# Graph attention on one core: a table fetch by product for every third step's eighth tile, and 64-row edge products

## What is computed

```python
q, k, v = x @ Wq + bq, x @ Wk + bk, x @ Wv + bv
e = eattr @ We
kj = k[src] + e
alpha = sum(q[dst] * kj, axis=-1) / sqrt(C)
a = exp(alpha - segment_max(alpha, dst)[dst])
a = a / (segment_sum(a, dst)[dst] + 1e-16)
out = segment_sum(a[..., None] * (v[src] + e), dst) + x @ Ws + bs
```

## Time and profile before

| | |
|---|---|
| median of 3 runs | 6819.26 us (6818.12 to 6822.41) |
| profiled execution | 6818.34 us, its span 6816.5 us |
| mean granted clock of TensorE | 0.538 of full speed |
| busy: PE, PEld | 4422.8 us (65%), 3475.0 us (51%) |
| busy: DVE, ACT, POOL | 4366.3 us (64%), 1118.9 us (16%), 4726.5 us (69%) |
| DMA | 675.79 MB, mean 99 GB/s |

### The profile page before, as it was taken

The page is one execution under the profiler, slowest core; times in us unless marked ns, Lnnn a source line. Parts: engine busy times, 40 slices in busy tenths (PEclk is TensorE's granted clock), DMA queues, the critical chain, the costliest instruction groups (busy, mean ns, idle before and its releaser), DMA issues. The chain is left out here.

```text
span 6816.5 us, 149747 instructions
## 1 busy us (share of the span) xinstructions
PE 4422.8 (65%) x36620; PEld 3475.0 (51%) x36620; DVE 4366.3 (64%) x15732; ACT 1118.9 (16%) x4722; POOL 4726.5 (69%) x5116
## 2 busy tenths in 40 slices
PE   7996666666666667666666666667666666666665
PEld 5775444444444446444444444446444444444444
DVE  5556666666666666666666666666666666666666
ACT  3222111111111112111111111112111111111111
POOL 1224777777777775777777777775777777777776
PEclk9995555555555555555555555555555555555555
DMA  4553333333333333333333333333333333333333
GB/s 128 159 159 96 95 95 95 96 95 95 95 96 95 96 95 98 95 95 95 95 95 95 95 95 95 95 96 97 95 95 95 95 95 96 95 95 95 96 96 80
DMA packets 687682, 675.79 MB, mean 99 GB/s; under 512 B 369234, under 2 KB 506388, under 8 KB 687636
## 3 DMA queue, kind: packets, MB, share of 16 engines
q0 software_dynamic: 161600, 320.52, 18.3%
q1 hardware_dynamic: 496944, 301.76, 16.3%
q10 hardware_dynamic: 29092, 52.97, 2.6%
HBM read 652.96 MB, written 21.67 MB: 99 GB/s over the span
## 5 line engine op out<-in xcount | busy, mean ns | idle before, releaser
L1621 POOL DMA_INDIRECT Gall<-KV,sdn x4848 | 4590.0, 947 | 1517.0 <-issue 1380.9
L754 DVE TENSOR_TENSOR kj<-Gall,pE 128x512 f32<-128x512 f32 x603 | 414.4, 687 | 1973.4 <-DMA Gall<-KV,sdn 1971.3
L963 PE MATMUL pG<-O,vals 128*66 128x42 f32 (+1 forms) x10736 | 1291.9, 308 | 0.7 <-ACTq L1242 0.7
L963 PEld LDWEIGHTS pG<-O,vals 128*66 128x66 f32 (+1 forms) x10736 | 1200.8, 223 | 47.4 <-ACT vals L1002 28.4
L948 PE MATMUL pY<-fw,Ob 128*42 128x6 bf16 (+1 forms) x4800 | 255.1, 176 | 1139.9 <-DVE cr L807 1139.9
L994 ACT ACTIVATE vals<-dd 128x16 f32<-128x16 f32 (+1 forms) x606 | 131.6, 217 | 4679.5 <-DVE dd L834 4671.0
L948 PEld LDWEIGHTS pY<-fw,Ob 128*42 128x42 bf16 x4800 | 220.4, 121 | 1192.9 <-issue 1192.9
L896 PE MATMUL pE<-bd,ea 128*128 128x256 f32 x1212 | 739.9, 714 | 13.6 <-PEq L1242 13.6
L955 PEld LDWEIGHTS pM<-Mb,OTs 42*128 42x128 bf16 x4800 | 176.3, 101 | 921.1 <-issue 921.1
L901 PE MATMUL pE<-bd,ea 128*128 128x256 f32 x1212 | 642.8, 634 | 0.0
L955 PE MATMUL pM<-Mb,OTs 42*128 42x6 bf16 (+1 forms) x4800 | 209.9, 163 | 514.2 <-DVE df L825 511.8
(11 more groups left out here) (223 smaller groups left out, 6539.9 us busy)
## 6 DMA issues: line engine op xcount, KB each, us to landing
db<-D SPq DMA_DIRECT2D x606, 256.0 KB
ea<-in_ea SPq DMA_DIRECT2D x606, 128.0 KB
Gall<-KV,sdn POOLq DMA_INDIRECT x4848
db<-D ACTq DMA_DIRECT2D x202, 256.0 KB, 3.5
qw<-QT SPq DMA_DIRECT2D x1818, 5.2 KB
dr<-in_dr SPq DMA_DIRECT2D x1212, 4.0 KB
ea<-in_ea SPq DMA_DIRECT2D x202, 64.0 KB, 3.3
sdn<-in_sdn SPq DMA_DIRECT2D x606, 12.0 KB
```

Source lines behind the costliest of these rows:

```text
L754: return e.tensor_tensor(kj[:, :, :], G[u][:, :, 0:64], pE[u][:, :].rearrange("p (j c) -> p j c", c=64), ALU.add)
L963: return e.matmul(out[0:AR, 0:W], vals[u][:, j, 0:AR], O[u][:, j, :], start=j == 0, stop=j == T - 1)
L1621: e.indirect_dma_start(G[u][:, j, :], None, kvtab, bass.IndirectOffsetOnAxis(ap=sdn[u][:, j:j + 1], axis=0)).then_inc(s_g[u], 16)
```

## The change

- The table rows of k and v stay in SBUF too: `rows_A` writes into `KVS` [128, 50, 128] f32 instead of `stg`, and the stores to DRAM read from there. Scratch of the setup lies in `KVS` to make room.
- For steps of slot 0 from step 3 on (`picks`), POOL leaves out the gather of tile 7. PE makes these rows: `oh` is, for each group ("quad") of four table tiles, a one-hot matrix of the 128 keys against the row number; its product with 512 columns of `KVS` is accumulated in `pG` over all 13 quads. The 13 are spread as 4, 4 and 5 over three steps (`p_gp`, between `aT` and `Me`; the quad of the last two tiles has 256 columns). `v_oh` makes the one-hot matrices a step ahead, and `v_sel` takes, at the start of the picked step, of the four tiles in `pG` the right one into `G`.
- The keys: the mean pass collects the eighth source column of each step in `srcT`; before the first attention pass it is transposed, made into 16-bit keys and stored in `K16`, and SP loads the key row of a pick into `kb`.
- `agg` sums into `pY` instead of `pG`, and `facc` waits for `aT`.
- Edge products in attention passes: four of 128 columns, each over 64 rows, the two row halves into different banks of PSUM, so that `kj` and `vj` read `pE` through another pattern.

```diff
+        self.quads = -(-self.tiles // 4)
...
+    order_q = list(range(QUADS - 2)) + [QUADS - 1, QUADS - 2]
+    PIECE = [QUADS // 3, QUADS // 3, QUADS - 2 * (QUADS // 3)]
+    FROM = [0, PIECE[0], PIECE[0] + PIECE[1]]
...
+    KVS = sb("KVS", [128, NT, 128])
...
-            if before_kv[c]:
-                e.wait_ge(s_kv[g], before_kv[c])
             e.wait_ge(own["P"], pP["mm", c])
-            e.activation(stg[:, g, 0:m, 0:128], kv_bank[c % 2][:, 0:128 * m].rearrange("p (t c) -> p t c", t=m),
+            e.activation(KVS[:, cells(c), :], kv_bank[c % 2][:, 0:128 * m].rearrange("p (t c) -> p t c", t=m),
                          ACT.Copy).then_inc(own["A"], 1)
...
-                "V": ["A kj", "A vj", "B fhi", "B fm", "B flo", "B cr", "Z OT", "A prod", "A alpha", "C d1", "C d",
-                      "Z cont", "Z last", "A flag", "A O", "B X", "B Mhi", "B Mm", "B Mlo", "B df", "C vals",
+                "V": ["A sel", "A kj", "A vj", "B fhi", "B fm", "B flo", "B cr", "Z OT", "A prod", "A alpha", "C d1", "C d",
+                      "Z cont", "Z last", "A flag", "A O", "Z oh", "B X", "B Mhi", "B Mm", "B Mlo", "B df", "C vals",
                       "D facc", "D acc", "A scan"],
-                "P": ["B Fb", "A q", "D agg7", "B Mn", "Z e", "A aT", "B Me"],
+                "P": ["B Fb", "A q", "D agg7", "B Mn", "Z e", "A aT", "A gp", "B Me"],
...
-                "V": ["C acc", "Z O", "Z OT"],
+                "V": ["C acc", "Z src", "Z O", "Z OT"],
...
+        first_pick = 2 + z.peel
+        pick_slot = first_pick % 3
...
+        sums = [pSumY, pSumY, pSumY] if att else [pG, pQ, pY]
...
+        def picks(s):
+            return s.slot == pick_slot and not (isinstance(s.i, int) and s.c < first_pick)
...
+        def v_src(e, s):
+            ge16(e, s_i, 1, s)
+            return e.tensor_copy(srcT[:, bass.ds(s.value(), 1)], sdn[s.slot][:, LAST:T])
...
+        def v_sel(e, s, inc, n):
+            u = s.slot
+            to = G[u][:, LAST, :]
+            e.tensor_scalar(quarter[:, :], sdn[u][:, LAST:T], 7, 3, ALU.logical_shift_right,
+                            ALU.bitwise_and).then_inc(sel_V, 1)
+            e.wait_ge(sel_V, sel_at(s, 0))
+            e.tensor_tensor(msk[:, :], ioq[:, :], quarter[:, :].to_broadcast([128, 4]),
+                            ALU.is_equal).then_inc(sel_V, 1)
+            e.wait_ge(sel_V, sel_at(s, 1))
+            after(e, "P", "gp", s - 1)
+            e.tensor_scalar(to, pPick[:, 0, :], msk[:, 0:1], None, ALU.mult).then_inc(sel_V, 1)
+            for k in range(1, 4):
+                e.wait_ge(sel_V, sel_at(s, k + 1))
+                i = e.scalar_tensor_tensor(to, pPick[:, k, :], msk[:, k:k + 1], to, ALU.mult, ALU.add)
...
+        def v_oh(e, s):
+            k = (s.slot - pick_slot) % 3
+            m, f = PIECE[k], FROM[k]
+            if k == 0:
+                e.wait_ge(s_k, s.times(16, 16 * (2 - first_pick // 3)))
+            return e.scalar_tensor_tensor(
+                oh[s.slot][:, 0:m, :], kb[:, :].unsqueeze(1).to_broadcast([128, m, 128]), prow[:, 0:1],
+                pQd[:, f:f + m].unsqueeze(2).to_broadcast([128, m, 128]), ALU.subtract, ALU.is_equal)
...
+                after(e, "P", "aT", s + 3)
...
-                return e.matmul(pE[u][:, 0:256], ea[u][:, 0:128], bd32[:, l, :], start=True, stop=True)
...
+                return edges(e, u, 0)
...
+        def edges(e, u, half):
+            for x in range(2):
+                c = pEhalf[u][x] + 128 * half
+                p = e.matmul(pEall[:, c:c + 128], ea[u][64 * x:64 * x + 64, 128 * half:128 * half + 128],
+                             bd32[64 * x:64 * x + 64, l, 128 * x:128 * x + 128], start=True, stop=True)
+            return p
...
+        def p_gp(e, s):
+            k = (s.slot - pick_slot) % 3
+            after(e, "V", "oh", s)
+            hold(e)
+            if k == 0 and picks(s):
+                after(e, "V", "sel", s)
+                hold(e)
+            for n in range(PIECE[k]):
+                q = order_q[FROM[k] + n]
+                m = min(4, NT - 4 * q)
+                p = e.matmul(pG[:, 0:128 * m], oh[s.slot][:, n, :],
+                             KVS[:, 4 * q:4 * q + m, :].rearrange("p t c -> p (t c)"),
+                             start=k == 0 and n == 0, stop=k == 2 and n == PIECE[k] - 1)
+            return p
...
+            e.dma_start(kb[:, :], K16[bass.ds(s.value(), 1), :].to_broadcast([128, 128])).then_inc(s_k, 16)
...
-            for j in range(T):
+            for j in range(T - 1 if picks(s) else T):
```

More of the change, by code:

```diff
@@ L21 @@
 SL = 4
+LAST = T - 1
 class Sizes:
@@ L123, in build @@
     dnarrow = Gall[:, B * T:B * T + B * T // 2].bitcast(I16)
+    srcT = sb("srcT", [128, 4 * KG])
+    kb = sb("kb", [128, 128], I16)
+    oh = [sb(f"oh{u}", [128, PIECE[2], 128]) for u in range(3)]
+    quarter = sb("quarter", [128, 1], I32)
+    msk = sb("msk", [128, 4])
+    prow = sb("prow", [128, 1])
+    ioW = sb("ioW", [128, W])
+    ioq = sb("ioq", [128, 4], I32)
     sdn = [sb(f"sdn{u}", [128, 3 * T], I32) for u in range(3)]
@@ L551, in query_A @@
             e.wait_ge(own["P"], pP["qs", c])
-            e.activation(stg[:, g, 0:m, 128:192], both[:, :, 0:64], ACT.Copy).then_inc(own["A"], 1)
+            e.activation(stg[:, g, 0:m, :], both[:, :, 0:64], ACT.Copy).then_inc(own["A"], 1)
             e.activation(SQ[:, cells(c), :], both[:, :, 64:128], ACT.Copy).then_inc(own["A"], 1)
@@ L1242, in missing, with made @@
             e.sem_inc(prog[k], m - n)
+        def made(s):
+            return not isinstance(s.i, int) or s.c >= first_pick - 3
         def vector_step(e, t, on):
@@ L1379, in tensor_step @@
                 missing(e, "P", t, "aT", "aT")
+            if made(at):
+                p_gp(e, at).then_inc(pP, 1)
+            else:
+                missing(e, "P", t, "gp", "gp")
             if "B" in on:
@@ L1532, in load_db, with load_keys @@
             e.dma_start(db[u][:, :], D16[bass.ds(b, 1), :].to_broadcast([128, T * 128])).then_inc((s_l if att else s_d)[u], 16)
+        def load_keys(e, s):
+            if not (isinstance(s.i, int) and s.c == first_pick):
+                after(e, "V", "oh", s - 4)
+                hold(e)
+            e.dma_start(kb[:, :], K16[bass.ds(s.value(), 1), :].to_broadcast([128, 128])).then_inc(s_k, 16)
         def load_rows(e, s, b, base):
@@ L1576, in sync_step @@
             load_rows(e, s, b, base)
+            if att and picks(s + 2):
+                load_keys(e, s + 2)
         def sync(e, ready):
@@ L1588, in sync @@
                     sync_step(e, At(i, c))
+            if att:
+                after(e, "V", "oh", At(n, 1 + z.peel))
+                hold(e)
+                e.dma_start(kb[:, :], K16[0:1, :].to_broadcast([128, 128])).then_inc(s_k, 16)
         def pool_step(e, s):
```

179 lines of the change are left out of this document (129 added, 50 removed).

## The result

On the chip on which the kernel before takes 6818.86 us (median of 4 runs, 6818.12 to 6822.41), the changed kernel takes **6609.18 us** (4 runs, 6607.14 to 6612.21). The ratio is 0.9692, 95% interval 0.968 to 0.9704: 209.7 us less. The forecast was 6578.4, range 6560 to 6640. The profiled execution took 6607.14 us, 211.2 less than the one of before.

A forecast was written before the change was run, and what follows sets the result against it. The prediction took POOL's issue of gathers to bound the attention passes. From 6819.3 us it took 251.9 for the removed gathers and added 11 for setup and the ends of passes: 6578.4 us, range 6560 to 6640.

The forecast's parts named there:

- What bounds, and what a gather is worth: Attention passes: POOL's gather issue sets the pace; 201 gathers fewer at 1.253 us each save 251.9 us.
- The ends: Setup and the start and finish of passes: additions of +11 us together, bounds 0 to +25.
- The openings of the second and third pass: Start of these passes: one or two `oh` on the way to the first `kj`, +1 us each.
- The drains: End of each pass: the last `gp` and `sel` stand in the open, +1 us for each of three passes.
- TensorE: Attention steps: PE work of 9.15 us, or 8.7 with faster edges, under the 9.60 us step, hidden behind POOL.
- The block: Fetch products in each step: 7.1 us at the lower clock, which was to rise within each block; taken at 4.15.
- the second rival: Attention steps: the clock alternates and PE sets the pace at 10.3 us a step, 7002 us in all; chance 0.08.
- Edge products: Attention steps on PE: 2.0 us as now if pairs follow one another, 1.0 less if they overlap; half the gain taken.
- DVE: Attention steps: its work grows from 6.8 us to 7.9 on average and 8.8 in a pick step, under 9.60.
- Clock: TensorE in attention passes: 128-row products raise the clock within each block; granted clock between 0.6 and 0.9.
- PE becomes the bound: Attention steps: with an alternating clock, PE work of 10.3 us exceeds the 9.60 us step, giving 7002 us; chance 0.08.

The follow-up runs named there:

- `edges_128`: The changed kernel with its four edge products over all 128 rows instead of 64: 9543.84 us on the third chip, ratio 1.0487 to before.
- `fetch_64_rows`: The changed kernel with fetch products over rows 0 to 63 of one-hot and table instead of all 128: 10100.29 us on the third chip, ratio 1.1097.

## Why the prediction was right, and where it was off

**What bounds, and what a gather is worth.** Right on the first chip, as its two traces show; no experiment ran there. 4647 gathers, idle time "issue", 1.251 us per gather, 9.60 us a step. 251.9 us were the gain to be had.

**The ends.** The step that failed: +11 us, measured 33. The openings of the second and third pass were put at +1 us each and cost +6.6 and +5.6. The sum counted the `oh` operations and not what `oh(0)` waits for, although the change puts the key load in SP's queue behind the row loads; the prediction set that load to 0 by its place in the loop ("needed four steps later") and did not look at the first one. The drains, at +1 each, cost +4.9, +5.8 and +5.7: a `sel` of 1.92 us, the last `gp`, and a new wait of PE for `sel0`, which was not priced. For the first pass the sum had +4 and +1 up to its first `kj`; the first gather starts 1.5 us later and the opening costs 3.2, 4.7 together, as foreseen. Inside the passes the slack left 5 to 7 us where the sum had nothing. With 40 in place of 11 the sum gives 6607, the profiled time.

**TensorE.** Right in the whole, off in the terms, and the errors offset one another, which is luck. Per step 8.4 us busy, foreseen 8.7 to 9.15. Edge products and `aT` were taken at the lower level in every step, 2.3 us; they take 0.78 and 0.31. The block averages 4.9 us and was taken at 4.15; where it begins at the lower level the rise comes some 5 us into it (0.50 until 3008, 0.63 to 3010), later than assumed, and the block takes 6.29 us. That is the condition of the second rival. It didn't become the bound because half of the blocks begin at 2.4 GHz: then the aggregation takes 1.15 us and the edges 0.71. The clock outlives the wait before `Mn` in about half of the steps. The Trainium skill, "TensorE: Matmul & The Clock Gate", "HAM oscillation", describes a loop in which the wait of every pass sends it back; the trace agrees for the other half only (202 of 402 blocks of four begin at 1.2 GHz).

**Edge products.** Taken halfway between 2.0 and 1.0 us. The new lines take 1.23 us at the lower level (the step at 2620.06) and 0.71 at the upper. The old ones span 2.07 us at the lower level, from 2999.24 to 3001.31 in the step before the one of the earlier trace rows. So the gain at an equal clock is 0.84 us of the 1.0 that was the bound. It lies off the path: `edges_128` gives it back without a loss, on a chip where something else bounds.

**DVE.** 7.8 us a step, foreseen 7.9. `oh` takes 743 to 865 ns, foreseen 730 to 870. `sel` takes 1.92 us, foreseen 1.3: its four operations on 128 columns from PSUM take 0.35 to 0.37 each, not 0.21 like `cont`. The waits for TensorE (262.3 and 214.4 us) are the delayed `Fb` and the fetch, and fall where DVE had waited for gathers.

**Clock.** That the rise hangs on the use of all 128 rows is shown by `fetch_64_rows`, the half-row counterpart, on the third chip. What it rests on inside the chip isn't.

**What the prediction could not see.** On the fourth chip the same change loses 7%, and with the keys ahead of the rows it loses 7.0% on the second and 5.3% on the third. That is the outcome of the rival "PE becomes the bound", through a different mechanism than it named: TensorE's results come late beside the gathers, POOL is idle 3800 us in the kernel before, and what is added to TensorE is paid for. Nothing in the trace of before on the first chip shows that. The gain of 3.1% was measured on the first chip alone.

## What to carry to other kernels

When a change trades work of the engine that paces for work of one with room, the steady state is easy to price; look as closely at the first turn (what does each new operation wait for, and behind what is that queued?) and at the drain. To learn whether a product costs clock, look at how many rows it uses and not only at how busy it keeps the engine. And time such a trade on more than one chip: the room that it uses may not be there.

## What the runs showed of the hardware that was not expected

- The same kernel takes 6819 us on one chip and 9100 to 9170 on four others. The gathers take as long (947 and 949 ns), the mean pass too; the difference lies where indirect gathers run beside TensorE, whose semaphore in the step shown comes 5 to 9 us after the modelled end (0.02 us on the first chip). Some of SyncE's register instructions take over 0.5 us there as well (515 of 4824, none on the first chip). Pauses of 4 to 11 us stand in the straight code of the node phase only while gathers are issued. Taking 201 gathers away gained 1.74 us each on the second chip.
- With TensorE 89% busy at 1.2 GHz the clock does not rise for f32 products of 512 columns over 64 rows (granted 0.50); over 128 rows it does (0.73 on the same chip).
- A block of four 128x512 f32 products takes 3.67 us at 2.4 GHz, 7.16 us at 1.2 (over 64 rows), and 6.29 with the rise near its end.
